# Attention units of an adaLN block on one core: ScalarE's casts of q and k placed anew among the exponentials, VectorE's reciprocal placed behind k's low half

## What is computed

```
h = layernorm(x) * (1 + ca) + sa
x = x + ga * attention(h)          # 16 heads of 128, causal, softmax
h = layernorm(x) * (1 + cb) + sb
x = x + gb * moe(h)                # router, 8 experts of two layers, top 2, shared expert, core path
```

```
k = W_K h ; q = W_Q h ; v = W_V h
scores = k q^T, masked, / sqrt(128)
attn = softmax(scores) ; z = attn v ; out += W_O z
```

## Time and profile before

| | |
|---|---|
| median of three timed runs | 803.14 us |
| the profiled execution | 803.85 us |
| its span, first to last instruction | 801.8 us |
| mean granted TensorE clock | 0.99 of full |
| busy: TensorE, VectorE, ScalarE, GpSimd | 777.2, 669.8, 620.2, 462.9 us |

### The profile page before, as it was taken

How to read it: one execution, slowest core, us unless ns; L and a number is a source line. 1 busy time by engine, 2 the same in 40 slices (tenths; PEclk the granted TensorE clock), 3 DMA queues, 4 the chain that set the end, 5 groups by cost and what they waited for, 6 DMA issues and landing times.

```text
span 801.8 us, 14365 instructions
## 1 busy us (share of the span) xinstructions
PE 777.2 (97%) x4700; PEld 690.5 (86%) x4700; DVE 669.8 (84%) x1649; ACT 620.2 (77%) x1449; POOL 462.9 (58%) x389
## 2 busy tenths in 40 slices
PE   7899899999999999999999999999999899989997
PEld 6789898899999999999999999999999677778786
DVE  4779998888888888888788888879898988786967
ACT  4787878778887788877888877887879868766974
POOL 2555355665556666555566655665445365577654
PEclk9999999999999999999999999999999999999999
DMA  7263233343223444323333333344222131112221
GB/s 269 62 172 70 64 91 93 94 104 88 65 67 68 101 106 115 82 66 77 86 95 93 93 92 76 90 106 124 69 67 66 47 119 54 53 40 68 71 101 53
DMA packets 47594, 70.53 MB, mean 88 GB/s; under 512 B 5537, under 2 KB 38465, under 8 KB 47393
## 3 DMA queue, kind: packets, MB, share of 16 engines
q1 hardware_dynamic: 47008, 68.81, 32.6%
q0 software_dynamic: 368, 0.81, 0.3%
q10 hardware_dynamic: 144, 0.00, 0.0%
HBM read 25.49 MB, written 2.17 MB: 34 GB/s over the span
## 4 chain that ended last, share of the span: by engine, by line
PE 67%; ACT 15%; DVE 11%; issue 4%; POOL 2%; DMA 1%; SPq 0%; DVEq 0%; POOLq 0%
PE M L753 10%; PE M L754 10%; PE M L752 10%; PE T L754 7%; PE T L752 7%; PE T L753 7%; PE S L752 4%; PE S L754 4%; PE S L753 4%; ACT PB L643 3%; ACT PB L692 3%; DVE S L1165 2%; ACT qk L707 1%; ACT pth L720 1%; PE M L858 1%
## 5 line engine op out<-in xcount | busy, mean ns | idle before, releaser
L643 ACT ACTIVATE PB<-S,nb 128x128 f32<-128x128 f32 (+3 forms) x256 | 134.0, 534 | 113.2 <-DVE nb L1165 113.1
L600 POOL TENSOR_TENSOR ptl<-ptl,pth 128x896 fp32r<-128x896 f32 x126 | 179.6, 1448 | 43.2 <-ACT pth L720 43.1
L588 POOL TENSOR_TENSOR X<-X,fb 128x512 f32<-128x512 f32 x64 | 83.1, 1299 | 79.1 <-DVE fb L1201 73.5
L692 ACT ACTIVATE PB<-PB,ri 128x256 f32<-128x256 f32 (+3 forms) x256 | 124.6, 583 | 5.0 <-DVE ri L1174 4.9
L1165 DVE CUSTOM_DVE_ANT_0 S<-S,cc 128x128 f32<-128x128 f32 (+3 forms) x256 | 117.7, 525 | 1.3 <-PE S L754 1.3
L1154 DVE TENSOR_TENSOR qk<-M,qk 128x512 fp32r<-128x512 f32 x108 | 74.6, 691 | 42.3 <-ACT qk L707 42.3
L1181 DVE STREAM_TRANSPOSE gab<-PB 128x256 f32<-128x256 f32 (+2 forms) x192 | 109.6, 623 | 0.1
L593 POOL TENSOR_TENSOR rt<-qk 128x128 f32<-128x128 f32 x84 | 38.8, 462 | 118.0 <-DVE qk L1154 118.0
L754 PE MATMUL M<-hh,W 128*128 128x512 f32 x222 | 87.9, 396 | 0.0
L753 PE MATMUL M<-hl,W 128*128 128x512 f32 x222 | 87.8, 396 | 0.0
L752 PE MATMUL M<-hh,W 128*128 128x512 f32 x222 | 87.1, 392 | 0.5 <-DVE hl L1140 0.5
(11 more groups left out here) (264 smaller groups left out, 2500.1 us busy)
## 6 DMA issues: line engine op xcount, KB each, us to landing
ptl<-gab SPq DMA_DIRECT2D x256, 160.0 KB, 3.1
stage<-in_wat SPq DMA_DIRECT2D x16, 512.0 KB, 5.1
gab<-scw SPq DMA_DIRECT2D x16, 256.0 KB, 3.2
tmp<-scw SPq DMA_DIRECT2D x16, 256.0 KB, 3.5
X<-in_x SPq DMA_DIRECT2D x3, 512.0 KB, 7.2
stage<-in_wfa SPq DMA_DIRECT2D x3, 512.0 KB, 4.8
out<-X SPq DMA_DIRECT2D x3, 512.0 KB, 2.6
X<-in_wmod SPq DMA_DIRECT2D x1, 1024.0 KB, 12.8
```

Source lines behind the costliest of these rows:

```text
L588: pool.tensor_tensor(X[:, a:a + 512], X[:, a:a + 512], fb[:, c2 * 512:c2 * 512 + 512], ALU.add).then_inc(s_y, 1)
L600: pool.tensor_tensor(pt_part(lo, c), pt_part(lo, c).bitcast(F32), pt_part(hi, c).bitcast(F32), ALU.subtract).then_inc(s_pl, 1)
L643: ins = act.activation(PB[:, P_OFF[i]:P_OFF[i] + w], PS[bk][:, a:a + w], ACT.Exp, bias=nb[:, i:i + 1], scale=-1.0, accum_out=sm[:, i:i + 1])
L692: act.activation(p, p, ACT.Copy, scale=ri[:, i:i + 1]).then_inc(s_P3, 1)
```

## The change

In the loop over units ri(u) moves behind k(u+1). On ScalarE, for the scores of units 2 to 62, the cast of q(u+1) comes ahead of all exponentials of unit u, pieces 0 and 1 follow, then the cast of k(u+1), then piece 2.

```diff
-        add(("S", i + 2), ("q", i + 3), ("ri", i + 2), ("k", i + 3), ("norm", i + 2))
+        add(("S", i + 2), ("q", i + 3), ("k", i + 3), ("ri", i + 2), ("norm", i + 2))
...
                     if kind == "q" and ev[1] >= 2:
-                        exps(ev[1] - 1, [1, 2])
-                elif kind == "ex" or kind == "S" and ev[1] < NU - 1:
+                        exps(ev[1] - 1, [1, 2] if ev[1] == 2 else [0, 1])
+                    if kind == "k" and ev[1] >= 3:
+                        exps(ev[1] - 1, [2])
+                elif kind == "ex" or kind == "S" and ev[1] < 2:
                     u = ev[1]
-                    exps(u, [0] if 1 <= u < NU - 1 else [0, 1, 2])
+                    exps(u, [0] if u == 1 else [0, 1, 2])
```

## The result

| | before | change |
|---|---|---|
| median of eight runs | 803.47 us | 806.25 us |
| profiled execution, its span | 803.85, 801.8 us | 804.76, 802.7 us |
| ratio of times, 95% interval | | 1.0035 (1.002 to 1.005) |
| first mask of unit 1 (VectorE) | 31.88 | 31.68 |
| first mask of unit 63 | 616.49 | 619.73 |

The account below looks back on a forecast made before the run. The ring of ScalarE and VectorE was taken to set the time at both ends of attention, TensorE in the middle. 803.85+2.5 (front)+2.2 (end) = 808.6 us by the profiled execution, taken as 808.0; range 803.2 to 811.0.

Parts of the forecast that it names:

- norm in a plain unit: Plain unit: normalization on ScalarE waits for the reciprocal's round trip, 3.04 us behind the first exponential, before 2.98; taken as +0.07.
- unit 2: Front: q(3) is late from low-clock matmuls, and piece 0 now stands behind its cast; norm +1.44 us.
- unit 3: Front: q(4) waits for h's low half, and the first exponential now comes behind q(4)'s cast; +0.80 us with norm's +0.07.
- unit 5: Front: norm waits for the reciprocal, which now stands behind the low half on VectorE; +0.61 us.
- unit 7: Front: unit with statistics whose loop is ended by ScalarE with a weight piece; +0.61 us.
- unit 8: Front: norm waits for the reciprocal, now behind the low half on VectorE; +0.61 us.
- enters the end, ring against TensorE: End of attention: q's cast must come first, so the first exponential follows the last score matmul's start by 2.20, before 1.09.
- the ring: ScalarE, VectorE, ScalarE waiting on each other; sets the time at both ends of attention, a little faster than TensorE in the middle.
- rival 4: Clock falls to 1.2 GHz after a 3.4 us stall ahead of q(8): +0.6 to +1.5, 808.6 to 809.5 us; chance 0.13.
- Rival 1: Faster: TensorE is the bound, the ring's lateness is swallowed, waits for k go; 802.4, 801.7 or 800 us; chance 0.09.
- Rival 2: No change: VectorE's idle time swallows the late reciprocal, or the low clock misses q(3); 803 to 805 us; chance 0.14.
- Rival 3: Front only: ring not 1.1 later at unit 52, end's loops hide in TensorE's; 805.7 to 806.5 us; chance 0.22.

Follow-up runs that it names:

- VectorE's part alone: Kernel before with only the reciprocal moved behind k's low half in units 2 to 62, ScalarE's order as before; 842.55 us in a single execution.
- run with early reciprocals: The change, but in units 5, 7, 8, 57 and 61 the reciprocal is ahead of k's low half as before; 803.89 us, ratio 1.0001.
- ScalarE's part alone: ScalarE's new order in all units, but the reciprocal stays ahead of k's low half as in the kernel before; 803.47 us, ratio 0.9989.
- middle-only run: The change in units 21 to 52 alone, the order of the kernel before elsewhere; 805.55 us, ratio 1.0015.
- old order where q is late: The change, but units 2, 3 and 7 keep the order of the kernel before; 803.88 us, ratio 1.0001.
- selected units: ScalarE's new order only in units 4, 6, 9 to 20 and 53 to 62, late reciprocal only in 10 and 12; rest as before; 800.86 us, ratio 0.9961.

## Why the prediction was right, and where its sizes were off

The side was right, the size too large: 808.0 forecast, 806.25 measured, 4.9 us over the median then known, against 2.8. That it came so near is in part luck, as told below. By its own steps, in the profiled execution (the start's 0.2 us taken off):

| step | forecast | measured |
|---|---|---|
| norm in a plain unit | +0.07 | +0.03 to +0.05, the loop +0.00 |
| k's low half | -0.92 | -0.95 |
| loops that VectorE ended | -0.47 | -0.51 (unit 10) |
| unit 2 | +1.44 | -0.17 |
| unit 3 | +0.80 | +0.73 |
| unit 4 | -0.19 | -0.32 |
| unit 5 | +0.61 | +0.54 |
| unit 7 | +0.61 | +2.28 |
| unit 8 | +0.61 | +0.32 |
| sum up to the masks of unit 10 | +4.02 | +3.37 |
| TensorE enters the middle | +2.5 | +2.1 |
| enters the end, ring against TensorE | +1.11 | +1.08 |
| end in all | +2.2 | +1.4 |
| masks of unit 63 | +4.7 | +3.4 |

- **What bounds.** Right: VectorE's part alone shows what a longer ring costs, and the run with early reciprocals shows that at both ends the time follows the ring (1.8 us come back in the front, 1.2 at the end). The middle stayed without a gap, as forecast.
- **The sign that failed, and luck.** I wrote that the prediction is wrong if the masks of unit 7 begin less than 1.5 us later than before. They begin 0.59 later (0.79 from the masks of unit 1), where the sum had 2.73. By that sign the account of the front was wrong. Unit 2 had been put 1.6 us too high and unit 7 1.7 us too low; the two errors cancel, so that the sum at unit 10 is off by only 0.65. Had unit 7 lost only what I had put there, the change would have come out near 804.6 us: an estimate, 806.25 less 1.67.
- **Unit 2, the step that failed.** I took the low clock on q(3) from one profile as if it belonged there. In the change's two profiles q(3) ran at full speed, its cast started without a wait (40.06), and nothing was lost: -0.17 in place of +1.44. The term exists: in the run with ScalarE's part alone, where the clock fell on the scores of unit 2 and q(3) was late, the loop of unit 2 was 1.2 us longer than before and 1.4 longer than in the change. But no profile without such a fall shows it.
- **Unit 7, a term put at nothing, and rival 4.** The sum charged unit 7 with the reciprocal alone. But q(8) waits for a new batch's h as q(4) does, and the first exponential now stands behind its cast; that wait, priced in unit 3, was left out here. At full clock it is worth 0.61 (ScalarE's part alone). In the change the clock fell on q(8) besides, +0.85; I forecast a stall of 3.4 us ahead of q(8), measured 3.06 idle, and gave the fall 0.13. It came in both profiles of the change. With the reciprocal, +0.82, that is the 2.28 of the loop. Unit 8's term is smaller (0.32): with the old order and a late unit 7, in the middle-only run, its loop is shorter by 0.28, and the reciprocal adds 0.6 to that. Rival 4's time, 808.6 to 809.5, did not come: it was added to my sum, with the 1.44 of unit 2 in it. The rule of the Trainium skill (TensorE: Matmul & The Clock Gate, "HAM oscillation — how this bites in real kernels"), that a long enough idle gap puts TensorE back to the lower clock, agrees with the trace in what happened. The trace does not show that the longer stall did it: with the middle alone changed the clock fell behind a stall of 2.03 us, while it was kept behind 2.11 in the kernel before and behind 2.36 in the run with the old order where q is late.
- **Units 5, 57, 61.** +0.53 to +0.59 each, forecast +0.61; taking the reciprocal back in units 5, 7, 8, 57 and 61 gave 3.1 us.
- **The end.** The way in was right (2.19 instead of 1.11 behind the score matmul). Mis-sized were the loops behind it: those with a weight piece were to give +0.28 and gave nothing, units 56 and 60 were to give -0.38 and gave -0.65. The plain loop's +0.07 was no more than a rounding of the round trip: norm is 0.04 later, and the loop as long as before.
- **Rival 1**, TensorE as the bound that swallows everything, is refuted; the stalls ahead of S(11) and S(13) went, as it said, but the earlier one ahead of q(8) grew, from 2.11 to 3.06 us. **Rival 2**, no change, falls by the interval, though its condition came true: the low clock did not meet q(3). **Rival 3**, a loss in the front only, gave 805.7 to 806.5 us, which holds the measured 806.25 better than my 808.0 does; the time alone would speak for it. It is refuted by the traces: TensorE enters the middle 2.1 later, the masks of unit 63 come 3.4 later, and the middle-only run loses 1.1 to 1.2 behind unit 20.

What stays open: where TensorE's clock falls. Every kernel here has a stall of about 2 us ahead of S(2) and one of 1.6 to 3.4 us ahead of q(8). The low clock came behind the first in three profiles, behind the second in four, at q(4) and q(8) in that of VectorE's part alone, and behind neither in that of the selected units. In all but that of VectorE's part alone, q(8) kept its clock where the fall had come behind S(2), and lost it in four of the five others; why, no run here shows. By the prices above about 0.6 of the 3.4 us may be due to where the clock fell (0.85 on q(8) in the change, 0.28 on q(3) before): an estimate from single profiles. No experiment moved the fall at will, and the time of the selected units (12 runs) holds what falls there were in them.

## What to carry to other kernels

An engine that is busy all the time need not be the one that sets the time: when its stalls are at both ends, look for the ring of other engines that enters and leaves the full stretch, and add up what each step does to that ring, unit by unit. A helper step that is cheap and waited for (here a reciprocal of 0.2 us) belongs ahead of work that nobody needs as soon; a cast belongs ahead of other work only where its matmul is done by then. So choose an order per unit by what that unit carries, and not one for all. And a low clock seen in one profile is not a property of the kernel: price the step with it and without it.

## What the runs showed that I had not expected

- Two VectorE steps in the wrong order, with ScalarE's order unchanged, cost 39 us (842.55, one execution, against 803.76). I had expected it from the sum. TensorE's busy time shows little of it: from 150 to 560 us it is lower by 12.3 us of 410, but it makes 2431 matmuls there and no longer 2583, nearly 6% fewer.
- The time at which attention's unit 1 begins varied from 30.4 to 34.8 us between profiles, and the part behind unit 63 took 183.0 to 185.3 us (span less the first mask there). The first is more than the effect to be measured, the second nearly as much.
- What the low clock costs depends on where it falls. On q(3) the old order lost 0.28 us (norm of unit 2 at 3.25 behind the exponential instead of 2.97), while ScalarE's new order lost 1.4 in the one run where the clock fell just ahead, on S(2). On q(8) both orders lost about the same, 0.85 and 0.9 us, though the old one does not hold up the first exponential. In eight of nine profiles it fell into the first 100 us of attention.
